# A decoder layer in fp32 pairs: the first normalisation turned by VectorE instead of TensorE

## What is computed

```
x = x + block_attention(layernorm(x))   # one head of 512, causal in blocks of 128 rows, softmax, W_out, b_out
x = x + cross(layernorm(x), ctx)        # 16 heads of 32, 64 keys per batch, silu(masked scores) @ v, Wo
x = x + ffn(layernorm(x))               # 512 -> 2048, exact gelu, -> 512
```

## Time and profile before

| | |
|---|---|
| median of 3 runs | 1264.19 us (1264.07 to 1264.53) |
| profiled execution | 1264.23 us |
| its span, first to last instruction | 1261.8 us |
| TensorE busy | 1249.1 us (99%) |
| VectorE busy | 662.7 us (53%) |
| ScalarE busy | 487.2 us (39%) |
| GpSimd busy | 243.7 us (19%) |
| granted TensorE clock | 1.000 in every slice |

### The profile page before, as it was taken

How to read it: one execution, slowest core, us unless ns; L and a number is a source line. 1 busy time by engine, 2 the same in 40 slices (tenths; PEclk the granted TensorE clock), 3 DMA queues, 4 the chain that set the end, 5 groups by cost and what they waited for, 6 DMA issues and landing times.

```text
span 1261.8 us, 15612 instructions
## 1 busy us (share of the span) xinstructions
PE 1249.1 (99%) x5785; PEld 1040.3 (82%) x5785; DVE 662.7 (53%) x1210; ACT 487.2 (39%) x888; POOL 243.7 (19%) x225
## 2 busy tenths in 40 slices
PE   9989999999999999999999999999999999999998
PEld 7878888888888888878888888888888888888887
DVE  7476868686868686865733333434424333434211
ACT  6246555555555555564322232222222322223221
POOL 2303232323232323258502001001001010010000
PEclk9999999999999999999999999999999999999999
DMA  8220202020202020316110010010100100100000
GB/s 296 88 63 13 76 14 75 13 76 12 75 12 75 12 75 12 125 46 220 52 67 1 1 67 1 1 66 0 51 15 0 66 0 0 66 0 0 34 1 34
DMA packets 40486, 60.04 MB, mean 48 GB/s; under 512 B 4224, under 2 KB 14464, under 8 KB 40448
## 3 DMA queue, kind: packets, MB, share of 16 engines
q1 hardware_dynamic: 40448, 59.53, 14.2%
HBM read 41.17 MB, written 18.35 MB: 47 GB/s over the span
## 4 chain that ended last, share of the span: by engine, by line
PE 55%; DVE 0%; issue 0%; DVEq 0%
PE bank L50 18%; PE bank L52 18%; PE bank L51 18%; DVE resid L1186 0%; DVEq L1185 0%
## 5 line engine op out<-in xcount | busy, mean ns | idle before, releaser
L1176 DVE TENSOR_TENSOR hid_lo<-gelu_out,hid_hi 128x512 fp32r<-128x512 f32 x128 | 97.5, 762 | 405.8 <-ACT gelu_out L1140 405.8
L50 PE MATMUL bank<-zT,w_parts 128*128 128x512 f32 x768 | 299.1, 389 | 3.4 <-DVE zT L155 1.8
L52 PE MATMUL bank<-zT,w_parts 128*128 128x512 f32 x768 | 298.8, 389 | 0.0
L51 PE MATMUL bank<-zT,w_parts 128*128 128x512 f32 x768 | 298.8, 389 | 0.0
L1136 ACT ACTIVATE hid_hi<-bank,small 128x512 fp32r<-128x512 f32 x128 | 88.3, 690 | 498.8 <-PE bank L52 498.8
L50 PE MATMUL bank<-w2p_hi,hid_lo 128*128 128x512 f32 x512 | 199.2, 389 | 0.0
L51 PE MATMUL bank<-w2p_lo,hid_hi 128*128 128x512 f32 x512 | 199.2, 389 | 0.0
L52 PE MATMUL bank<-w2p_hi,hid_hi 128*128 128x512 f32 x512 | 199.2, 389 | 0.0
L50 PEld LDWEIGHTS bank<-zT,w_parts 128*128 128x128 f32 x768 | 144.2, 188 | 34.4 <-issue 2.3
L51 PEld LDWEIGHTS bank<-zT,w_parts 128*128 128x128 f32 x768 | 144.2, 188 | 29.9
L52 PEld LDWEIGHTS bank<-zT,w_parts 128*128 128x128 f32 x768 | 144.1, 188 | 29.8
(11 more groups left out here) (142 smaller groups left out, 1808.8 us busy)
## 6 DMA issues: line engine op xcount, KB each, us to landing
x_in<-in_x SPq DMA_DIRECT2D x32, 256.0 KB, 3.5
x_dram<-resid SPq DMA_DIRECT2D x32, 256.0 KB, 2.1
w_raw<-in_w SPq DMA_DIRECT2D x32, 256.0 KB, 3.3
resid<-x_dram SPq DMA_DIRECT2D x32, 256.0 KB, 3.8
out_dram<-resid SPq DMA_DIRECT2D x32, 256.0 KB, 2.1
resid<-in_wqkvT SPq DMA_DIRECT2D x12, 256.0 KB, 5.2
mask_i<-in_mask SPq DMA_DIRECT2D x16, 128.0 KB, 2.7
values_now<-values_dram SPq DMA_DIRECT2D x8, 256.0 KB, 2.8
```

The source lines that it names most:

```text
L50: pe.matmul(out_ap, lhs[1], rhs[0], start=start, stop=False)
L51: pe.matmul(out_ap, lhs[0], rhs[1], start=False, stop=False)
L52: return pe.matmul(out_ap, lhs[0], rhs[0], start=False, stop=stop)
L1176: dve.tensor_tensor(hid[1][:, c % 4, :], gelu_out[:, c % 2, :], f(hid[0][:, c % 4, :]), ALU.subtract).then_inc(hid_lo, 1)
```

## The change

The first normalisation of the next tile is made one step ahead: its x rows are loaded a second time, into the free buffers of the feed-forward weights (`ahead`), the rows are normalised at the start of step (a, b) for tile a + 1, VectorE turns them in sixteen transposes of 32x32 squares spread over the step into `z1_cols`, and at the start of the next step ScalarE and VectorE split `z1_cols` where they split PSUM banks before. `transposed_chunks` is called for tile 0 alone. Banks are numbered anew. On GpSimd the bias additions come first in a step and wait for the new rows. In step 1 the low keys come ahead of the rows. The low queries, mask and low values change places on VectorE, and TensorE waits for each low query by itself. In the set-up the fold begins with its high products, its two waits on its own end go, the warm-up has eight matmuls and starts behind half a memset, the rows of tile 1 are loaded ahead of chunk 12, and VectorE makes their statistics. VectorE's and GpSimd's last two steps are written out. SyncE's scratch size goes from 4096 to 2048.

```diff
-WARM_UP = 9
+WARM_UP = 8
-VALUE_BANK = (1, 2, 3, 4)
-SELF_BANK = (0, 7)
-SCORE_BANK = (0, 1, 2, 3, 5, 6, 7, 0)
+VALUE_BANK = (5, 6, 7, 0)
+SELF_BANK = (4, 3)
+SCORE_BANK = (4, 5, 6, 7, 1, 2, 3, 4)
...
+            def load_ahead(sp, n):
+                for i in range(NB):
+                    sp.dma_start(ahead[i], x_blocks[n * NB + i, :, :]).then_inc(ahead_loaded[i], 16)
+
+            def stats_ahead(dve, n, blocks):
+                for i in blocks:
+                    dve.wait_ge(ahead_loaded[i], 16 * n)
+                dve.nop(nofuse=True)
+                for i in blocks:
+                    dve.bn_stats(stats1[:, i, :], ahead[i]).then_inc(ln1[0], 1)
...
@@ set-up, SyncE
                                 for i in range(NB):
                                     load_x(sp, 0, i)
+                                load_ahead(sp, 1)
@@ set-up, VectorE, behind the splits
+                        stats_ahead(dve, 1, range(NB))
+                        aggregate(dve, 1, mv1, ln1)
                         dve.wait_ge(bias_loaded, 64)
@@ set-up, GpSimd
-                        for blocks in (kb_lo, kb_hi, *vb):
-                            pool.memset(f(blocks[:, :, :]), 0.0).then_inc(filled, 1)
+                        for blocks in (kb_lo[:, 0:EC, :], kb_lo[:, EC:PAIRS, :], *(part_[:, :, :] for part_ in (kb_hi, *vb))):
+                            pool.memset(f(blocks), 0.0).then_inc(filled, 1)
@@ fold
+                                pe.wait_ge(split_hi, n + 2)
+                                for m in range(EC):
+                                    pe.matmul(bank[banks + m][:, :], part[0][:, n % PARTS, cols(m)],
+                                              part[0][:, (n + 1) % PARTS, :], start=c == 0, stop=False)
                                 pe.wait_ge(split_lo, n + 2)
...
-                                if c == EC - 1:
-                                    pe.wait_ge(done, 1)
-                                    pe.sem_inc(part_used, 1)
@@ attention, SyncE's step
+                            if twice_more(a):
+                                sp.wait_ge(z1_ready, NB * (a + 2))
+                                load_ahead(sp, a + 2)
@@ attention, GpSimd's step
-                            if b is not None:
-                                norm_rstd(pool, mv1, ve1, rstd1, ln1, a)
-                                for j in range(4):
-                                    silu_low(b, j)
-                            pool.wait_ge(z1_ready, NB * (a + 1))
+                            if more(a):
+                                pool.wait_ge(z1_ready, NB * (a + 2))
                             for i in range(NB):
+                                pool.wait_ge(x_loaded[i], 16 * (a + 1))
                                 pool.tensor_tensor(x_in[:, i, :], x_in[:, i, :], bout_row[:, :], ALU.add
                                                    ).then_inc(x_biased, 1)
...
                             norm_rstd(pool, mv2, ve2, rstd2, ln2, a)
+                            if twice_more(a):
+                                norm_rstd(pool, mv1, ve1, rstd1, ln1, a + 2)
@@ attention, ScalarE's step
-                                for m in range(EC):
+                                for m in range(EC - 1):
                                     q_high(b, m)
-                                for c in range(EC):
-                                    chunk_high(act, a, c, 4)
+                                act.wait_ge(z1_turned, TURNS * a)
+                                act.wait_ge(q_done, EC * (b + 1))
+                                z1_high(0)
+                                q_high(b, EC - 1)
+                                for c in range(1, EC):
+                                    z1_high(c)
@@ attention, VectorE's step
-                                start_step(b, mv1, rstd1, ln1, a)
-                                for m in range(EC):
-                                    q_low(b, m)
-                                for c in range(EC):
-                                    chunk_low(dve, a, c, 4)
+                                start_step(b)
+                                if more(a):
+                                    rows_ahead(a + 1, b)
+                                q_low(b, 0)
+                                q_low(b, 1)
                                 mask_now(b)
+                                q_low(b, 2)
                                 values_low(b)
+                                z1_low(a, 0)
+                                q_low(b, EC - 1)
+                                for c in range(1, EC):
+                                    z1_low(a, c)
                                 dve.wait_ge(mask_ready, b + 1)
-                                for j in range(4):
+                                for j in range(3):
                                     mask_scores(b, j)
+                                dve.wait_ge(z1T_lo, EC * (a + 1))
+                                dve.nop(nofuse=True)
+                                turn(a, 0, 2)
+                                mask_scores(b, 3)
+                            else:
+                                rows_ahead(1, None)
+                                dve.wait_ge(values_stored, 16 * BATCH)
+                                dve.nop(nofuse=True)
+                                turn(a, 0, 2)
+                            turn(a, 2, 2)
...
@@ the other turns: 4 behind y low 2, 5 to 8 behind y low 3, 9 and 10 behind the first half of the
@@ self scores, 11 and 12 behind the softmax bias, then:
+                            turn(a, 13, 2)
                             dve.wait_ge(pT_hi, a + 1)
...
                             for i in range(NB):
+                                if i == 1:
+                                    turn(a, 15, 1)
                                 if b is not None and i in (1, 2):
                                     o_low(b, i + 1)
                                 dve.bn_stats(stats[:, i, :], x1_rows(i, par)).then_inc(ln2[0], 1)
...
-            next_stats(dve, a + 1, (0, 1))
+            stats_ahead(dve, a + 2, (0, 1)), and (2, 3) with their aggregates behind the lows of z2
@@ attention, TensorE's step
                                 queries(b, range(EC))
-                                transposed_chunks(pe, a, 4)
+                                if not first(b):
+                                    pe.wait_ge(x2_ready, NB * b)
                                 pe.wait_ge(kv_ready, len(BLOCKS) * b + HEADS_PER_CHUNK)
                                 for m in range(2):
-                                    pe.wait_ge(q_lo, 2 * (EC * b + 2 * m + 2))
+                                    pe.wait_ge(q_lo, 2 * (EC * b + m + 1))
                                     cross_scores(m)
...
-                                if c == 0:
-                                    pe.wait_ge(z1T_lo, EC * a + m + 1)
+                                if m == 0:
+                                    pe.wait_ge(z1T_lo, EC * a + c + 1)
+                                if c == 0 and b is not None:
+                                    pe.wait_ge(q_lo, 2 * (EC * b + m + 1))
```

More of the change, by code:

```diff
@@ L199, in second_residual, with squares @@
                               ).then_inc(x2_ready, 1)
+        QUADS = P // SQUARE
+        TURNS = QUADS * QUADS
+        def squares(n, to):
+            row, col = divmod(n, QUADS)
+            taken = zn[cols(row, SQUARE), :, :].rearrange("p i (c q f) -> p i c q f", c=EC, q=QUADS)
+            put = to[cols(col, SQUARE), :, :].rearrange("p c (i q t) -> p i c q t", i=NB, q=QUADS)
+            return put[:, :, :, row, :], taken[:, :, :, col, :]
         layer = ExitStack()
@@ L229, in decoder_layer_program @@
             values_stored, wo_lo = sem("values_stored"), sem("wo_lo")
-            values = [w2_raw[:, b, :] for b in range(STAGES)]
-            values.append(w1_raw[:, 0, :, :].rearrange("p c n -> p (c n)"))
+            z1_cols = sb("z1_cols", [P, EC, TILE])
+            values = [z1_cols[:, b, :] for b in range(BATCH)]
+            ahead = [w1_raw[:, i, :, :].rearrange("p c n -> p (c n)") for i in range(STAGES)]
+            ahead.append(w2_raw[:, 0, :])
+            ahead_loaded, z1_turned = [sem(f"ahead_loaded{i}") for i in range(NB)], sem("z1_turned")
             RAWS = 2 * NB
@@ L492, in first, with more, twice_more @@
                     return isinstance(t, int) and t == 0
+                def more(a):
+                    return not (isinstance(a, int) and a == TILES - 1)
+                def twice_more(a):
+                    return not (isinstance(a, int) and a >= TILES - 2)
                 with nc.Block() as block:
@@ L566, in step @@
                             if b is not None:
-                                for j in range(4, 8):
+                                for j in range(8):
                                     silu_low(b, j)
@@ L578, in last_step @@
                                 silu_low(b, j)
```

(33 more changed lines are left out.)

87 lines of the change are left out of this document (48 added, 39 removed).

## The result

The changed kernel takes 1276.64 us (median of four runs, 1274.77 to 1276.87), the kernel before 1264.13 beside it: a ratio of 1.0096, 95% interval 1.0084 to 1.0108. I had forecast 1266.1, in a range of 1261.3 to 1269.0. The four runs of the kernel before lie 0.8 us apart; those in the table ahead of the prediction lie 0.46 apart, not "fewer than three tenths". All of this is small beside 12.5. The profiled execution is the fastest of the four, 1274.77 us with a span of 1272.9, so 1.87 us lie outside the span, against 2.43 before.

The account below looks back on a forecast made before the run. TensorE, busy 99% of the span, was taken to bound the kernel. Against 1264.23 us, 3.9 + 3.75 + 3.0 + 0.1 + 1.5 - 10.4 = +1.85 gave 1266.1 us, range 1261.3 to 1269.0.

Parts of the forecast that it names:

- Saved on TensorE, 1.74 in each of six steps: Steps 2 to 7: sixteen transposes leave TensorE, saving 10.4 us in all; bounds 1.66 and 1.75 a step.
- Set-up, +3.9: Set-up: tile 1's load (2.6 us) and VectorE's statistics and aggregates (2.85, 1.6 absorbed) make step 0 start 3.9 us late.
- move only TensorE, which then waits at the boundary: nothing: Set-up: shorter fold waits, eager high products and the earlier, shorter warm-up were to gain nothing.
- Steps 0 and 1, +3.75: Longer VectorE chains: low probabilities +1.5 in step 0, y products late in step 1; +3.0 together, plus 0.75 from the port.
- The port, 0.6 in steps 2 to 6: GpSimd's additions and VectorE's mask conversion share an SBUF port: TensorE restarts 0.6 us late each step, 3.0 in all.
- End of step 6, +1.5: GpSimd's additions collide with VectorE's rows of the second normalisation; TensorE 0.9 to 2.2 us late once, taken as 1.5.
- taking turns: End of step 6: rows and GpSimd's additions alternate, so the rows end at 271.0 to 272.3 instead of 268.5.
- both gaps: TensorE idle for 3.4 us at the boundary ahead of step 0 and 3.7 us in step 1.
- rival 3: TensorE's clock falls to the 1.2 GHz level in a gap, a loss of 2.9 us: 1269.0 us; chance 0.10.

Follow-up runs that it names:

- e10: The changed kernel with everything in e9, and VectorE's steps 2 to 5 written out as well; 1252.07 us, ratio 0.9905 to the kernel before.
- e11: The kernel before with only the new order of the folds in the set-up; 1262.87 us, ratio 0.9992.
- e2: The changed kernel with the mask conversion moved behind the last low of z1 in steps 1 to 7; 1271.32 us.
- e3: The changed kernel with GpSimd's four bias additions back behind the first four silu lows, waiting for no rows; 1268.94 us.
- e7: The changed kernel with the four normalised rows of tile 2 put ahead of the low keys, in step 1 only; 1276.56 us.
- e1: The changed kernel with squares 13 and 14 of step 0 put ahead of the last value low; 1273.40 us.
- e8: The changed kernel with eight thrown-away matmuls ahead of each of two TensorE waits, in step 0 and step 1; 1272.33 us.
- e4: The changed kernel with VectorE's steps 2 to 5 written out instead of looped, no operation moved; 1273.17 us.
- e9: The changed kernel with e1, e2, e3 and e7 together, and the load and statistics of tile 1 later; 1254.02 us, ratio 0.9920.

## Why the prediction was wrong

The sum was +1.85 by profile and the profile says +10.54. What failed above all is point 6, the clock, with point 7 beside it. By its own steps:

1. **Saved on TensorE, 1.74 in each of six steps.** Right in kind. Free of waits, a step takes 61.52 (e10) against 63.13: 1.61, just below my lower bound.
2. **Set-up, +3.9.** Measured +3.03. The load was right (2.6 against 2.58; that it agrees to hundredths is luck), the statistics 1.25 against 1.67. What was wrong is "move only TensorE, which then waits at the boundary: nothing": the fold order is worth 1.2 us (e11), and some 0.5 of it is seen where VectorE's last addition waits for TensorE. The total came close since the errors have opposite signs.
3. **Steps 0 and 1, +3.75.** The waits came as told: 3.17 for the low probabilities (forecast 3), 3.30 before the y products (3 to 4). Without the clock the sum holds: of 3.91 + 1.14 + 2.62 = 7.67, what the clock cost is 18 slow matmuls of 0.2 us, 3.6, which leaves 4.1 against 3.75.
4. **The port, 0.6 in steps 2 to 6.** The mechanism was right and shown by moving either side of it (e2, e3), and in a third place by e7. The size: steps 2, 3 and 5 took 62.19 to 62.53 where I had 62.0.
5. **End of step 6, +1.5.** The collision was found at its place; the rows end 3.85 us late, just above the 2.5 to 3.8 that I had for taking turns, and TensorE lost 2.1 in three waits (0.51, 0.76, 0.84), all gone in e3.
6. **The clock.** This is the step that failed. I foresaw both gaps (3.4 and 3.7 us), and rival 3 had the right mechanism, but at a chance of 0.10, and I wrote that it "decides from the gap that lowers the level, which no row shows". A mechanism with gaps almost twice as long as any in the old stream needed an even chance at least; behind gaps of 3.2 to 3.3 us it struck 18 times out of 20. And it was priced once, 2.9 us. It could strike at four places, the boundary, step 0, step 1 and step 4, and in the profile did at the last three: 26 slow matmuls, 5.2 us at 0.2 each. The mean granted clock is 0.995 in the profiled run and 0.993 in the other three, which took 1.9 us longer. e1 and e2 show a fall at the boundary; that this is the missing 1.9 is inferred, since those three runs have no profile. That the clock goes with the spread is seen elsewhere: e8's runs took 1271.0 and 1271.2 us at a mean clock of 0.997 and 0.998, and 1273.4 and 1273.5 at 0.994.
7. **Not in the sum at all:** VectorE's jump back to the start of its loop, 2.0 us in step 4. It made the wait there 2.53 and so gave the clock one more chance to fall: 65.89 us for the step, 3.7 more than its neighbours. In e4's profile all of that is gone.

By the stretches of the first table, measured less forecast: set-up -0.87, step 0 +1.51, step 1 -0.21 and +2.62, step 4 +3.90, step 6 +1.33, the other four steps +1.01 together, the rest -0.60: 8.69, the whole miss of the profiled run. The clock's 5.2 and the jump's 2.0 are most of it. The squares themselves fitted in as forecast: in e10, with everything else in place, a step has no wait left.

## What to carry to other kernels

Work that leaves a full engine for one with gaps is a gain only as long as the full engine's own gaps do not grow: look first for those that the change lengthens, and count for a long one its length and, at the odds below, what TensorE's matmuls lose behind it. When an addition on GpSimd is moved, list what VectorE reads from SBUF under it, in the ordinary step and in the last one. And sum the parts one by one: here 1.6 us a step was a real gain, hidden under mistakes of placement, most of which could be undone.

## What the runs showed of the chip

In the fourteen profiles of this case, between the warm-up and the feed-forward block, TensorE waited 42 times for 1.0 to 1.77 us, and matmuls at the 1.2 GHz level never followed; 16 times for 1.83 to 1.98, and 4 times they did; 9 times for 2.53 to 2.82, 5 times; 20 times for 3.17 to 3.32, 18 times. The same wait behind unchanged code went either way from one profile to the next, and one kernel's runs spread over up to 3.9 us. One fall was 6 to 8 matmuls at 0.43 instead of 0.23 us, about 1.5 us, or 11 to 14 of them, about 2.5. They began at once or up to 1.6 us after the wait's end.

VectorE's jump to the head of its loop paused it for 2.0 us with a body of 222 operations (2.3 in e9), and not visibly with 188. And an engine that "only waits at the end" can still hold up others: folds that ended earlier made the whole kernel 1.2 us shorter.
